# Adding the causal mask on VectorE while taking the row maxima of two attentions

## The reference

```python
# attention A
att = einsum('bthd,bThd->bhtT', q, k) / sqrt(8)
att = where(causal, -inf, att)              # keys after the query are left out
att = softmax(att, axis=-1)                 # needs the maximum of every row
# attention B
scores = where(tril, einsum('btghk,bThk->bghtT', qg, k), -inf) / sqrt(64)
p = softmax(scores, axis=-1)
```

## Time and profile before

| | us |
|---|---|
| median of three runs (533.77 to 535.16) | 534.98 |
| the profiled execution's own time | 533.74 |
| its span, first to last instruction | 531.9 |
| TensorE busy, 2980 matmuls | 462.6 |
| VectorE busy, 1023 instructions | 368.0 |
| ScalarE busy | 229.1 |
| GpSimd busy | 161.7 |
| mean granted TensorE clock | 0.968 |

### The profile page before, as it was taken

One profiled execution on the slowest core, in us unless ns is written; L12 is line 12 of the kernel. 1 busy time (PEld: TensorE's weight loads), 2 busy tenths in 40 slices (PEclk: granted clock), 3 DMA queues, 4 the chain that ended last, 5 costly groups with the idle time before them and its releaser, 6 DMA issues.

```text
span 531.9 us, 8374 instructions
## 1 busy us (share of the span) xinstructions
PE 462.6 (87%) x2980; PEld 259.6 (49%) x2980; DVE 368.0 (69%) x1023; ACT 229.1 (43%) x418; POOL 161.7 (30%) x200
## 2 busy tenths in 40 slices
PE   3877976899999999999999999999988969888930
PEld 2544533455365555735563655445344427565620
DVE  3634789947777786788579777847984536655785
ACT  1262531754474175337443742654243330545531
POOL 4311130510423132225303331403403646061542
PEclk9987899999999999999999999999999999899985
DMA  7600000000021003000300120030080162023224
GB/s 207 201 2 2 1 3 0 3 1 1 4 49 33 2 4 81 1 2 3 81 1 4 32 50 2 5 81 0 7 234 2 44 155 97 1 76 100 62 68 99
DMA packets 19095, 23.95 MB, mean 45 GB/s; under 512 B 2630, under 2 KB 15374, under 8 KB 18158
## 3 DMA queue, kind: packets, MB, share of 16 engines
q1 hardware_dynamic: 15308, 18.29, 12.8%
q0 software_dynamic: 1648, 4.07, 2.8%
q10 hardware_dynamic: 2098, 1.05, 0.7%
HBM read 16.81 MB, written 6.28 MB: 43 GB/s over the span
## 4 chain that ended last, share of the span: by engine, by line
PE 65%; DVE 17%; issue 5%; DMA 5%; ACT 5%; POOL 2%; ACTq 1%; POOLq 0%; DVEq 0%
PE ps_r L1003 7%; PE ps_r L1027 7%; PE ps_st L968 5%; PE ps_r L715 5%; PE ps_st L1273 4%; PE ps_r L773 4%; PE ps_r L873 4%; DMA xs_dram<-x_all,sidx 3%; PE ps_st L957 3%; PE ps_r L1016 3%; PE ps_r L850 3%; DVE rmax_a L1371 2%; PE ps_r L823 2%; PE ps_r L982 2%; PE ps_r L832 2%
## 5 line engine op out<-in xcount | busy, mean ns | idle before, releaser
L606 POOL TENSOR_TENSOR qkr<-qkr,prod 128x512 f32<-128x512 f32 (+1 forms) x48 | 52.3, 1095 | 182.9 <-DVE prod L1497 182.7
L1371 DVE TENSOR_REDUCE rmax_a<-ps_r 128x2 f32<-128x512 f32 (+1 forms) x96 | 62.2, 686 | 46.1 <-PE ps_r L850 45.9
L1371 DVE TENSOR_REDUCE rmax<-ps_r 128x2 f32<-128x512 f32 (+1 forms) x96 | 62.4, 685 | 16.7 <-PE ps_r L982 12.4
L715 PE MATMUL ps_r<-cbt 128*128 128x256 bf16 (+1 forms) x192 | 60.7, 316 | 3.6 <-ACT xT_b L1969 1.1
L1954 ACT ACTIVATE pt<-ps_st 128x1024 f32<-128x1024 f32 x48 | 46.9, 1018 | 35.9 <-PE ps_st L968 35.9
L643 POOL TENSOR_TENSOR oT<-pvb,oT 128x1024 f32<-128x1024 f32 x14 | 32.8, 2369 | 67.9 <-DMA oT<-inv_dram 67.9
L1945 ACT ACTIVATE pt<-ps_st 128x1024 f32<-128x1024 f32 x48 | 46.5, 1024 | 12.7 <-PE ps_st L757 12.5
L2015 ACT ACTIVATE pvb<-ps_r 128x512 f32<-128x512 f32 x32 | 19.0, 596 | 72.8 <-PE ps_r L1003 72.6
L1003 PE MATMUL ps_r<-pt,vb 128*64 128x512 f32 x192 | 48.2, 608 | 2.3 <-ACT pt L1954 2.0
L1027 PE MATMUL ps_r<-wqkv,xT_b 128*128 128x512 f32 x96 | 48.1, 605 | 1.0 <-DVE prod L1497 0.5
L715 PEld LDWEIGHTS ps_r<-cbt 128*128 128x128 bf16 x192 | 18.4, 96 | 48.9 <-issue 32.8
(11 more groups left out here) (238 smaller groups left out, 869.3 us busy)
## 6 DMA issues: line engine op xcount, KB each, us to landing
oT<-inv_dram SPq DMA_DIRECT2D x14, 512.0 KB, 5.7
xs_dram<-pvb SPq DMA_DIRECT2D x1, 2048.0 KB
pt<-in_L_ffn_w SPq DMA_DIRECT2D x2, 1024.0 KB, 7.4
ys_dram<-qkr SPq DMA_DIRECT2D x14, 128.0 KB, 1.9
qkr<-xs_dram POOLq DMA_DIRECT2D x4, 256.0 KB, 3.8
x_all<-in_L_attn_x ACTq DMA_DIRECT2D x1, 896.0 KB, 8.9
pvb<-xs_dram POOLq DMA_DIRECT2D x3, 256.0 KB, 4.9
out<-x_all SPq DMA_DIRECT2D x1, 640.0 KB, 3.8
```

What stands on the lines that cost most here:

```text
L606: nc.gpsimd.tensor_tensor(part, part, prod[:, (3 * t + i) % 2, 0:w], ALU.add).then_inc(add_in, 1)
L715: nc.tensor.matmul(o[:, :, P * (i >= 4):], ident_b, qmask.unsqueeze(1).broadcast_to([P, heads, P]), start=True, stop=False, skip_group_che ...
L1371: nc.vector.tensor_reduce(heads_of(i), ps_r[:, b, :].rearrange("p (h k) -> p h k", h=4 if i < 4 else 2), AX.X, ALU.max).then_inc(free[b], 1)
```

## The change

The mask products of both attentions' maxima are gone: `mask_rows` becomes `max_bank`, which only waits for the bank, and the score product starts the accumulation itself. VectorE replaces the one reduction of a bank by one `tensor_tensor_reduce` for each head: it adds the mask to the head's 128x128 or 128x256 scores, writes the sum back to PSUM in place, and takes the maximum over it, starting from -3e30. The bank is released by the last of them. For the second query tile the mask must be 256 wide, a block of zeros followed by `qmask`, so the bf16 table gets a block of zeros in front of `qmask`. To make room, the small tile `tmap` moves into a part of a tile that is free late. The masks of the second pass are untouched.

```diff
-    b = np.concatenate([np.eye(P), add_row, by_query, by_key, np.ones((P, P)), tri, top_row, by_strip], 1)
+    b = np.concatenate([np.eye(P), add_row, np.zeros((P, P)), by_query, by_key, np.ones((P, P)), tri, top_row, by_strip], 1)
...
+        both_masks = cbt[:, CB_BOTH:CB_BOTH + T]
...
-        tmap = sb("tmap", [P, sum(COUNT)], mybir.dt.int32)
+        tmap = late[:, 800:800 + sum(COUNT)].bitcast(mybir.dt.int32)
...
-            def mask_rows(s, name, i):
-
-                o = fill(s, name)
-                heads = 4 if i < 4 else 2
-                o = o.rearrange("p (h k) -> p h k", h=heads)
-                nc.tensor.matmul(o[:, :, P * (i >= 4):], ident_b, qmask.unsqueeze(1).broadcast_to([P, heads, P]),
-                                 start=True, stop=False, skip_group_check=True)
-                return o
+            def max_bank(s, name, i):
+
+                return fill(s, name).rearrange("p (h k) -> p h k", h=4 if i < 4 else 2)
...
-                    nc.tensor.matmul(o, q, k, start=False, stop=True, skip_group_check=True).then_inc(full, 1)
+                    nc.tensor.matmul(o, q, k, start=True, stop=True).then_inc(full, 1)
...
-                    nc.vector.tensor_reduce(heads_of(i), ps_r[:, b, :].rearrange("p (h k) -> p h k", h=4 if i < 4 else 2),
-                                            AX.X, ALU.max).then_inc(free[b], 1)
+                    to, heads, mask = heads_of(i), *((4, qmask) if i < 4 else (2, both_masks))
+                    o = ps_r[:, b, :].rearrange("p (h k) -> p h k", h=heads)
+                    for h in range(heads):
+                        ins = nc.vector.tensor_tensor_reduce(o[:, h, :], o[:, h, :], mask, 1.0, 3 * NEG, ALU.add, ALU.max,
+                                                             to[:, h:h + 1])
+                    ins.then_inc(free[b], 1)
```

More of the change, by code:

```diff
@@ L187 @@
 CF = CF_PLACES + sum(COUNT)
-CB_ID, CB_ADD, CB_QMASK, CB_KMASK, CB_ONES, CB_TRI, CB_TOP = (P * i for i in range(7))
-CB_STRIPS = 7 * P
+CB_ID, CB_ADD, CB_BOTH, CB_QMASK, CB_KMASK, CB_ONES, CB_TRI, CB_TOP = (P * i for i in range(8))
+CB_STRIPS = 8 * P
 CB = CB_STRIPS + 4 * P
@@ L846, in form_maxima_a @@
                 for i in range(lo, hi):
-                    o = mask_rows(s, f"am{i}", i)
+                    o = max_bank(s, f"am{i}", i)
                     q, k = (qs[:, i, 0:P], ks[:, :, 0:P]) if i < 4 else \
                         (qs[:, (i - 4) // 2, P:], ks[:, 2 * (i % 2):2 * (i % 2) + 2, :])
-                    nc.tensor.matmul(o, q, k, start=False, stop=True, skip_group_check=True).then_inc(full, 1)
+                    nc.tensor.matmul(o, q, k, start=True, stop=True).then_inc(full, 1)
             def max_rows_a(s, t):
@@ L974, in maxima @@
                 for i in range(lo, hi) if "MB" in stages(s) else ():
-                    o = mask_rows(s, f"bm{i}", i)
+                    o = max_bank(s, f"bm{i}", i)
                     if i < 4:
@@ L978, in maxima @@
                             mm = nc.tensor.matmul(o[:, 2 * j:2 * j + 2, :], qhi[1 - u][:, 2 * i + j, 0:P],
-                                                  kdiag[1 - u][:, j, :, 0:P], start=False, stop=j == 1,
-                                                  skip_group_check=True)
+                                                  kdiag[1 - u][:, j, :, 0:P], start=True, stop=True)
                     else:
                         mm = nc.tensor.matmul(o, qhi[1 - u][:, i - 4, P:], kdiag[1 - u][:, i % 2, :, :],
-                                              start=False, stop=True, skip_group_check=True)
+                                              start=True, stop=True)
                     mm.then_inc(full, 1)
```

## The result

The changed kernel takes **556.04 us** (median of 4 runs, 554.7 to 557.0) where the kernel before takes 534.38 (4 runs, 533.25 to 535.16): ratio **1.0405**, 95% interval 1.0371 to 1.044. That is 19 us over the predicted 537.1 and outside the range. The profiled execution has a span of 553.5 us against 531.9.

What follows compares the result with a forecast made beforehand. TensorE was taken to bound the full steps, VectorE the ends. Ends +4.6, four locked steps -1.0, first full step -1.2, step at 348.5 -0.3: +2.1 us, 537.1 us median; range 530 to 554.

Steps and rivals of the forecast that it cites:

- What bounds the kernel: TensorE bounds the long middle, busy 48.73 of 49.0 us in a full step; VectorE leads at the ends.
- the likeliest case: The prediction's own case, a little slower: 536.6 to 543 us, chance 0.35.
- fixed cost: Rival: VectorE's reducing instructions take 0.26 and 0.39 us, or their accumulator read isn't covered; about +16 us, 551 us; chance 0.14.
- VectorE's price: Reducing instructions 0.21 and 0.345 us apart, so a bank costs 0.25 or 0.09 us more; 27.5 us over all banks.
- the part behind the end of GpSimd's product: Full step after 216.6 us: VectorE's later banks use up TensorE's savings, except the last two masks; -0.25 us a step.
- The serial end: Each reducing instruction waits out the one before and its read, 0.37 or 0.50 us; as a rival 585 us, chance 0.05.
- TensorE's saving: Removed mask products give TensorE back 31 us in all, 3.9 us in a full step with both attentions.
- The lock: In a full step VectorE's small L1454 ends with GpSimd's product (L643), so the 0.7 us won before it is lost.
- The ends: Opening stretches and routing step, where VectorE's added work delays TensorE: together +4.6 us.
- The routing step: The chain runs over the last banks of maxima, bm6 to bm11, to the slots and scatter: +0.7 us.
- the sign that it named for a full step: Full step expected at 48.7 us; under 48, lock or ring held less; over 50, VectorE's price was higher.

Runs made afterwards that it cites:

- the trials: Changed kernel with runs of VectorE instructions added behind its last layer norm, source, destination, mask and operation varied: 0.249 us apart writing PSUM, 0.212 writing SBUF (reducing, 128 elements).

## Why the prediction was wrong

**What bounds the kernel: right.** TensorE has no slack in the full step of the kernel before (masks twice: +3.45 us), and VectorE sets the opening. The sign was right (slower had 0.54 in all), the size was not: 556 us lies outside the likeliest case (536.6 to 543, with 0.35) and inside the bounds of "fixed cost" (543 to 560, with 0.14).

**VectorE's price: mis-sized, and the step that failed.** The sentence is "I take the lower end, because the mean square's rows are the same instruction and writing is what their neighbours do at the same pace". The mean square reduces and writes SBUF (0.21 us); its neighbours in the earlier trace rows read PSUM, write SBUF as well and don't reduce (0.20). In the trials writing PSUM alone costs nothing (0.20), reducing alone 0.21, and both together 0.25. The term of 27.5 us was 46.7. The operand taken at no change, the bf16 mask, was free as said. In the full step it was the part behind the end of GpSimd's product that went wrong: forecast at -0.25 us, it gained 1.2 (35.0 to 36.2), while the part in front stood nearly still (14.0 to 14.2). That the forecast price would have given the forecast step is an estimate: between one instruction a bank (1.2 us more of VectorE a step, 47.5 us) and the changed kernel (5.8 more, 50.5), the 3.4 us forecast come to 48.9.

**The serial end** (0.37 and 0.50 us) did not occur: the next instruction starts with the read, not behind it. The rival "fixed cost per instruction" had 0.26 and 0.39 us from "VectorE: DVE Perf Modes" of the Trainium skill, section on the TRN2 errata, and 551 us; measured are 0.25, 0.38 and 556. As a number the page was the better guide, by luck: from PSUM to SBUF, the case that it describes, the trials show 0.21 and 0.345.

**TensorE's saving: right as a price, wrong as a gain.** 3.9 us were counted a step. 3.45 come when they are added once more, and 1.9 when they are taken away with VectorE unchanged, because the chain then partly leaves TensorE (11.2 us of VectorE on it, 4.6 before), the lock of about 1 us included.

**The lock: misplaced.** "So whatever TensorE and VectorE win between the reciprocal and 216.6 only lengthens L1454" was read from the lock's own rows. It was a real lock and the profile after shows it as forecast, 1.38 us and ending with GpSimd. But in the four full steps of the kernel before nobody on the chain waited for it: the earlier trace rows, quoted for another purpose, run from 210 to 219 us over TensorE alone, past its end. With the change it came onto the chain and costs 0.9 to 1.5 us a step, a part of what VectorE's price takes below. As a cap on a gain it is borne out in part: without masks, where the step does fall, it is on the chain. The full step, forecast at 48.7, is 50.5: from 49.0, the masks' leaving gives 1.9 (47.1), and VectorE's price takes 3.4; 1.3 of the 50.5 go if the lock goes.

**The ends: right in place, three times too small.** The opening was forecast at 1.5 + 0.5 + 0.5 + 0.3 + 1.1 = 3.9 us and is 11.8. nm1, forecast at 26.9, stands at 28.2. By its own price the prediction should have found more: VectorE's 11.0 us of added work there scale to 11.0 x 27.5 / 46.7 = 6.5 us, and I gave only the parts before a visible wait of TensorE, as if idle time took the rest. It took next to none (11.0 us of added work, 11.8 late), though the clock fell too. Of the miss of 19 us some 8 lie in the opening, 9 in the steps and 3 behind them. The routing step and what lies around it were forecast at 0.7 and are +3.8 from the start of transposed values at 349.2 to the slots; its six last banks alone go from 3.68 to 4.69 us (427.33 to 432.02).

**Of what was to be seen in the profile after:** the pitches were 0.25 and 0.38 (forecast 0.21 and 0.345), VectorE busy 410.7 (395), TensorE 462.1 (400, for the reasons given with the page of the profile), and the sign that it named for a full step "over 50, VectorE's price was higher" is what happened.

## What to carry to other kernels

Price an instruction by a row that has its operation, its accumulator and its destination together; two rows that each have one of them don't add up to it, and where none has it the forecast should not stand on one of the bounds (here 0.25 us came, between 0.21 and 0.37). A lock or a wait matters only where the chain passes, so read the chain past its end before using it as an anchor, and ask again which waits come onto the chain when another engine takes the lead. Work moved to an engine with a quarter of its time free can still cost more than it saves: here 46.7 us of VectorE were paid for at most 31 of TensorE, and each bank needs both engines in turn.

## What the runs showed of the hardware

- A reducing instruction of VectorE that writes PSUM starts its successor 0.037 us later than one that writes SBUF (0.249 against 0.212 us at 128 elements, 0.381 against 0.345 at 256), and the read of its accumulator takes 0.14 instead of 0.08 us; the first of a run is spared. Reading PSUM makes no difference, and a plain tensor_tensor pays nothing for writing it (0.20 us).
- Some of VectorE's small SBUF instructions stand still until GpSimd's product ends: the `tensor_scalar` of L1454 (0.17 us alone, 1.30 and 1.38 beside it, 0.17 with the product shortened), and a `tensor_tensor` with both inputs in SBUF (L1328, 0.15 us alone, 1.16 beside it in the run without masks). Others pass at their usual pace beside it: `bn_stats` and `bn_aggr` from SBUF (0.28 and 0.15 to 0.18 us), a `tensor_tensor` with one input from PSUM (0.29), reductions from PSUM (0.68). "SBUF — State Buffer" of the Trainium skill, section "SBUF: two separate sides", says that the two engines share a pair of ports, which one of them holds for a whole instruction, VectorE only for certain modes or with two SBUF inputs. These traces agree for the two SBUF inputs; the mode of the `tensor_scalar` they don't show.
- In the opening TensorE's granted clock is 0.93 before and 0.82 after over the stretches above, that is more time at the lower of its two levels, 1.2 GHz. It is also 0.85 in the run without masks, where VectorE's work is as before and TensorE only has less to do, and 0.93 with TensorE's masks twice. What brings the clock down, no run here separates.
